# One-core decoder layer: the sixteen stores of row numbers, one after every second routed tile

## The reference

```python
x = layernorm(x + attention(x))                    # 16 heads, causal
x = layernorm(x + chosen_expert(x, token_ids))     # 4 experts, one per token, by token id
x = layernorm(x + routed_ffn(x))                   # below

def routed_ffn(x):                                 # x: 2048 tokens x 512
    probs = softmax(x @ Wr)                        # 8 experts
    weights, selected = top_k(probs, 2)
    moe = sum over the 2 selected e of weight * ((silu(x @ Wg[e]) * (x @ Wu[e])) @ Wd[e])   # 352 wide
    shared = sigmoid(x @ Wsg) * ((silu(x @ Sg) * (x @ Su)) @ Sd)                             # 1408 wide
    return moe + shared
```

## Time and profile before

| | us |
|---|---|
| three runs | 1273.8, 1274.9, 1279.4; median 1274.9 |
| profiled execution, its own time | 1270.91 |
| its span in the trace | 1269.2 |
| PE busy | 1185.3 (93%) |
| DVE, ACT, POOL busy | 687.3, 454.4, 281.5 |
| routed tiles: first and last turning of x | 785.99, 1054.96 |
| stores of row numbers: first and last issue | 806.8, 827.3 |

### The profile page before, as it was taken

How to read it: one execution, slowest core, us unless ns; L and a number is a source line. 1 busy time by engine, 2 the same in 40 slices (tenths; PEclk the granted TensorE clock), 3 DMA queues, 4 the chain that set the end, 5 groups by cost and what they waited for, 6 DMA issues and landing times.

```text
span 1269.2 us, 20255 instructions
## 1 busy us (share of the span) xinstructions
PE 1185.3 (93%) x6404; PEld 934.3 (74%) x6404; DVE 687.3 (54%) x1485; ACT 454.4 (36%) x699; POOL 281.5 (22%) x405
## 2 busy tenths in 40 slices
PE   7788999999899879999999999889999998999996
PEld 6565676576476558887688888779999997778884
DVE  5574556656557546765467435234344433676744
ACT  3244434434435322322333333234444533233331
POOL 3012313412514311223002530410000000443302
PEclk8889999999999979999999999989999999999998
DMA  7237564532423224334124673555435432655530
GB/s 246 75 101 236 177 226 132 146 91 51 141 62 123 76 100 129 121 116 134 49 87 136 227 259 108 88 101 182 133 125 186 149 107 67 197 173 169 174 117 33
DMA packets 128814, 169.76 MB, mean 134 GB/s; under 512 B 18112, under 2 KB 71360, under 8 KB 128704
## 3 DMA queue, kind: packets, MB, share of 16 engines
q1 hardware_dynamic: 113056, 132.45, 34.9%
q0 software_dynamic: 10336, 32.53, 7.2%
q10 hardware_dynamic: 5312, 3.42, 1.2%
HBM read 95.98 MB, written 47.19 MB: 113 GB/s over the span
## 4 chain that ended last, share of the span: by engine, by line
PE 44%; DMA 3%; DVE 2%; POOL 1%; issue 1%; ACT 1%; SPq 1%; DVEq 0%; ACTq 0%; POOLq 0%
PE bank L908 17%; PE bank L847 16%; PE bank L1528 3%; PE bank L1529 3%; PE bank L1530 3%; DMA routed_wdraw<-in_L_ffn_Wd_dram 1%; PE bank L1550 1%; DMA routed_gu_raw<-in_L_ffn_Wg_dram 1%; PE bank L1573 1%; POOL routed_rows_io L1443 1%; SPq L1326 0%; DVE shared_held L1847 0%; PE bank L1480 0%; DMA routed_rows_io<-sorted_y,routed_pos 0%; DVE acc L1936 0%
## 5 line engine op out<-in xcount | busy, mean ns | idle before, releaser
L908 PE MATMUL bank<-store,shared_held 128*128 128x512 f32 x792 | 188.0, 393 | 4.3 <-issue 2.9
L908 PEld LDWEIGHTS bank<-store,shared_held 128*128 128x128 f32 x792 | 149.0, 189 | 39.4 <-DVE shared_held L1847 5.0
L482 PE MATMUL psT<-store 128*128 128x512 f32 x576 | 159.2, 412 | 5.3 <-DVE store L696 3.5
L782 DVE CUSTOM_DVE_ANT_0 psS<-psS,attn_mask 128x512 f32<-128x512 f32 (+3 forms) x256 | 120.9, 510 | 62.1 <-PE psS L548 62.1
L652 ACT ACTIVATE acc<-psE 128x512 f32<-128x512 f32 x160 | 93.7, 598 | 142.0 <-PE psE L569 138.3
L482 PEld LDWEIGHTS psT<-store 128*128 128x128 f32 x576 | 106.7, 197 | 25.6 <-issue 4.0
L424 POOL TENSOR_SCALAR_AFFINE_SELECT acc<-acc 128x256 f32<-128x256 f32 (+1 forms) x160 | 57.2, 364 | 274.7 <-ACT acc L652 274.3
L847 PE MATMUL bank<-shared_held,routed_h_hi 128*128 x624 | 116.0, 328 | 0.6 <-DVE routed_h_lo L1888 0.3
L1443 POOL DMA_INDIRECT routed_rows_io<-sorted_y,routed_pos x32 | 37.2, 1163 | 298.2 <-DMA sorted_y<-routed_rows_io 233.8
L847 PEld LDWEIGHTS bank<-shared_held,routed_h_hi 128*128 128x128 f32 x624 | 100.3, 188 | 2.0 <-issue 1.8
L847 PE MATMUL bank<-store 128*128 x351 | 93.2, 410 | 0.0
(11 more groups left out here) (273 smaller groups left out, 2022.1 us busy)
## 6 DMA issues: line engine op xcount, KB each, us to landing
sorted_x<-attn_zero SPq DMA_DIRECT2D x19, 768.0 KB, 6.4
shared_raw<-in_L_ffn_Sg_dram SPq DMA_DIRECT2D x44, 256.0 KB, 3.0
shared_raw<-in_L_ffn_Su_dram SPq DMA_DIRECT2D x44, 256.0 KB, 3.3
shared_raw<-in_L_ffn_Sd_dram SPq DMA_DIRECT2D x44, 256.0 KB, 4.4
routed_rows_io<-sorted_x SPq DMA_DIRECT2D x39, 256.0 KB, 2.9
sorted_y<-routed_rows_io SPq DMA_DIRECT2D x39, 256.0 KB, 3.0
attn_qS<-attn_ch_hi SPq DMA_DIRECT2D x128, 64.0 KB
attn_kS<-attn_ch_hi SPq DMA_DIRECT2D x112, 64.0 KB
```

What stands on the lines that cost most here:

```text
L482: last = pe.matmul(out, lhs[a](k), rhs[c](k), start=(s[-1] == 0 and k == 0), stop=(s[-1] == 2 and k == KC - 1))
L782: last = dve.tensor_tensor_reduce(scores, scores, mask[:, (3 - t) * P:T], 1.0, BELOW_ALL, ALU.add, ALU.max, rowmax[:, g % 2, t, i:i + 1])
L908: last = pe.matmul(out, w[:, slot, at + k * P:at + (k + 1) * P], x_part(k), start=(g == 0 and k == 0), stop=(g == 2 and k == KC - 1))
```

## The change

The one wait ahead of the sixteen stores becomes a wait ahead of each. Store t is issued when 4 + 2t routed tiles have been turned: the first at 4, as before, the last at 34 of the 39. The stores, their order, their data, the wait for all of them and the load back are the same.

```diff
-            pool.wait_ge(x_turned, 4)
             for t in range(NT):
+                pool.wait_ge(x_turned, 4 + 2 * t)
                 pool.indirect_dma_start(out=token_rows, out_offset=bass.IndirectOffsetOnAxis(ap=place[:, t:t + 1], axis=0),
                                         in_=number[:, t:t + 1], in_offset=None).then_inc(ids_out, 16)
             pool.wait_ge(ids_out, 16 * NT)
```

## The result

The changed kernel is slower. Ten executions have a median of 1287.0 us (1283.1 to 1296.2), ten of the kernel before one of 1279.4 (1273.8 to 1283.4): a ratio of the means of 1.0081, 95% interval 1.0051 to 1.0112, about 10 us (the medians lie 7.6 us apart). The forecast was 11.5 us less.

A forecast was written before the change was run, and what follows sets the result against it. PE was taken to bound the kernel (93% busy), standing still at the first change of expert. 12.5 - 0 - 1.0 = 11.5 us saved, from 1274.9 to 1263.4 us; range 1258 to 1269.

The forecast's parts named there:

- The loss at the first change of expert: Routed tiles, turnings 5 to 9: 12.5 us lost beside the burst of stores, all to come back.
- The price of a store: Stores beside the traffic held up: 1.0 us of all the DMA engines for each.
- the bound from above: Burst of sixteen stores, 34.1 us from first issue to last landing: at most 2.1 us each.
- Stores a tile ahead of the down weights: Five changes of expert with down weights issued 6.7 us after a store: no cost counted.
- The two places that I did price at 1.0 us in sum: Down weights meeting a store at turnings 6 and 20: at most 2.1 us, half taken, 1.0 us.
- The store beside gate and up weights: Store at turning 4: x tile 1.0 us later, 3.0 us left over, cost 0.
- the rival "half": First change of expert: one store already makes most of the lateness; saving 6 us, 1268.9 us; chance 0.07.
- my sign against the forecast: First change of expert: gate load still over 10 us beside one store would mean no change or half.
- The x and y transfers, POOL's queue and `token`: Other stores beside x loads and y stores, and POOL up to the first gather: cost 0.
- The slower rival: Spread stores hurt where they land: at 8.8 us each, 27.2 us lost, a time of 1289.6; chance 0.04.
- its four places: Slower rival: two down-weight loads pay d each, x tiles at turnings 4 and 18 what exceeds 4.0 us.
- My argument against it: Against the slower rival: sixteen stores landed in 34 us beside 3.87 MB, which could not be at 8.8 each.

The follow-up runs named there:

- e1: Sixteen stores of row numbers and the load back left out, against the kernel before: ratio 0.9838, turning 5 to 39 in 229.9 us.
- g4: The kernel before, unchanged, profiled a second time: 1282.5 us, turning 5 to 39 in 247.3 us.
- e3: Fifteen stores ahead of the routed tiles and a single one at turning 10, against the kernel before's block at turning 4: 1269.9 us, turning 5 to 39 in 232.7.
- the early block: All sixteen stores and the load back ahead of the scatters of rows, before the routed tiles, against the kernel before: ratio 0.9892.
- f1: The kernel before, its block of sixteen stores at turning 4, with table entries 512 bytes apart: ratio 1.0009, turning 5 to 39 in 247.0 us.

## Why the prediction was wrong

*The loss at the first change of expert* (12.5 us, from the rhythm of the turnings) was right for the trace it was read from, and the stores were its cause: e1 gives it all back. As the usual loss it was too small: g4 has 17.8. And in g4 it has another mechanism, the hold of ACT, which that trace doesn't show.

*The price of a store* is the step that failed. I divided the train's cost by sixteen: 1.0 us each, and as the bound from above 34.1 us over 16, 2.1 each. But landings in a train overlap. Sixteen together kept the others slow for some 30 us once; singly each is in flight for its own 7 to 12 us, and slows what is loaded in that time: one load followed took 7.16 us for 4.1. The bound from above was a bound for a store in a train and none for one alone. The row for the latter was there, 8.8 us for the first store, and I gave it to a rival with 0.04. (Two slips beside it moved nothing: 2 x 1.03 should be 2 x 1.0, and by their own weights the chances add up to 0.855 for faster and 0.105 for the same.)

*Stores a tile ahead of the down weights* I counted as free, because they had been issued 6.7 us before. A store lands 9.8 us after its issue (median), so it was still at work. Five of seven changes have that phase. e3 shows it alone: 3.0 us. The two places that I did price at 1.0 us in sum cost 1.7 (tile 6 to 7) and next to nothing (20 to 21).

*The store beside gate and up weights* was to have 3.0 us of cover and cost nothing. At turning 4 the x tile landed 15.0 us after its issue, where I had 8.0; PE waited 3.9 us for it, and the tile took 4.1 too many. At turning 18 it was 2.1. The gate weights held ACT as long as in the train of sixteen. This is what the rival "half" said of a first store, and my sign against the forecast, a gate load of over 10 us, came true (12.7 us from issue to split).

*The x and y transfers, POOL's queue and `token`* were costed at nothing, rightly: the first gather still waits for y stores, 47.7 us behind the load back, and the part behind turning 39 takes 214.2 us in both traces.

*The slower rival* had the mechanism: a store holds the other queue for d us, with a net loss beyond d = 5.1, 27.2 us lost at 8.8 and +14.7 in all. The tiles lost 30.6 us against the undisturbed rhythm. That the sums are close is luck: its four places cost 7.9 us, and the other 22.7 were lost at the five changes that it too had put at nothing. My argument against it, that sixteen landed in 34 us, is the division again.

The accounts come near in the tiles: 259.0 - 247.3 (g4) = 11.7 us more, beside 10 us in the timed runs, with one trace each, both of executions above their median. The first trace gives 16.8, and 7.6 of the 24.3 us between the two profiled executions lie ahead of turning 5, where the two kernels don't differ.

## What to carry to other kernels

The mean cost of a transfer in a train says nothing about one alone: latency that overlaps in a burst is paid each time when the burst is spread, and what spreading saves at one place it can charge to every tight place. Before moving such a store, ask how long it is in flight and which loads with no slack start in that time, also those issued after it; and first look whether it can be made cheap (entries 16 bytes apart gave 229.2 us in one trace, and 512 bytes apart 0.988 when timed) or stand where everything beside it has slack (0.989), and look again there: the early block, which seemed free in the tiles, cost up to 8.6 us ahead of them in one trace. And one profiled execution that lies 6 us below the timed ones is a reason for a second trace, before its stall is taken as the usual one.

## What the runs showed of the hardware that I had not expected

- An indirect store of 128 entries of 4 bytes, side by side in DRAM in a few runs, takes a median of 9.8 us to land, and slows the other DMA queue meanwhile (a load took 7.16 us for 4.1 beside one); the same entries 16, 64 or 512 bytes apart land in 3.7, 3.4 and 3.4 us.
- Beside a train of fifteen or sixteen indirect stores from POOL (some 20 us) engines stood though nothing that they needed was late by the records: in three traces ACT alone, for 15.6 to 18.4 us, with 1.4 MB of weights issued by SP within 0.7 us of the train's start; in two ACT and DVE, for up to 5.2 us, without them. Four traces with such a train show no such wait. In f1 SP's table reads rose from 272 to 694 ns meanwhile.
